# A recommendation tower (embedding gathers, pair products, three-layer MLP) on one core: GpSimd's gather loop unrolled, ids read in place, gathers released by pairs of feature groups

## What is computed

```python
e = jnp.stack([tbl_0[ids[:, 0]], tbl_1[ids[:, 1]], ..., tbl_25[ids[:, 25]]], axis=1)
combined = jnp.concatenate([dense[:, None, :], e], axis=1)         # (2048, 27, 128)
interactions = jnp.einsum('bfd,bgd->bfg', combined, combined)
iu, ju = jnp.triu_indices(27, k=1)
z = jnp.concatenate([dense, interactions[:, iu, ju]], axis=1)
h = jnp.concatenate([z, dense], axis=1)
h = jnp.maximum(h @ W_top1 + b_top1, 0.0)                          # 607 -> 512
h = jnp.maximum(h @ W_top2 + b_top2, 0.0)                          # 512 -> 256
y = h @ W_top3                                                     # 256 -> 1
```

## Time and profile before

| | |
|---|---|
| median of 3 runs | 739.69 us (738.09 to 743.75) |
| profiled execution, span | 741.8 us |
| TensorE matmuls busy | 462.5 us (62%), 3102 matmuls |
| VectorE, ScalarE busy | 240.0 us (32%), 271.2 us (37%) |
| GpSimd busy | 296.8 us (40%), 310 of its 317 instructions gathers |
| DMA | 34.56 MB, mean 47 GB/s |

### The profile page before, as it was taken

The page is one execution under the profiler, slowest core; times in us unless marked ns, Lnnn a source line. Parts: engine busy times, 40 slices in busy tenths (PEclk is TensorE's granted clock), DMA queues, the critical chain, the costliest instruction groups (busy, mean ns, idle before and its releaser), DMA issues.

```text
span 741.8 us, 9097 instructions
## 1 busy us (share of the span) xinstructions
PE 462.5 (62%) x3102; PEld 426.3 (57%) x3102; DVE 240.0 (32%) x697; ACT 271.2 (37%) x629; POOL 296.8 (40%) x317
## 2 busy tenths in 40 slices
PE   1327837482927649286683867658395592854987
PEld 1317727372927649175582857548294582842886
DVE  3216335240614215151331614315053340401441
ACT  2218322351605424062330714217051360614763
POOL 6760636345270543606245071622607147172000
PEclk9756958695967959578595886859677695875997
DMA  5564114211122111301012010230102212010000
GB/s 145 160 190 44 45 31 67 54 30 42 30 59 34 39 32 35 65 19 46 25 46 74 6 50 14 61 59 19 52 4 64 52 30 53 8 54 21 2 1 0
DMA packets 25437, 34.56 MB, mean 47 GB/s; under 512 B 9248, under 2 KB 18976, under 8 KB 25418
## 3 DMA queue, kind: packets, MB, share of 16 engines
q0 software_dynamic: 9920, 20.34, 10.3%
q1 hardware_dynamic: 15498, 13.97, 9.4%
HBM read 34.27 MB, written 0.01 MB: 46 GB/s over the span
## 4 chain that ended last, share of the span: by engine, by line
PE 52%; issue 26%; another core or an unknown queue 9%; ACT 7%; DMA 3%; DVE 2%; SPq 0%; ACTq 0%; DVEq 0%
PE gram_ps L428 17%; PE x_ps L411 15%; PE x_ps L388 4%; ACT x L608 4%; PE tail_ps L470 4%; PE tail_ps L472 3%; PE tail_ps L471 3%; DMA x<-in_tbl_dram 3%; PE tail_ps L501 2%; ACT gram L608 1%; PE tail_ps L464 1%; PE tail_ps L452 1%; DVE pairs L814 1%; ACT pairs L608 1%
## 5 line engine op out<-in xcount | busy, mean ns | idle before, releaser
L336 POOL DMA_INDIRECT rows<-in_tbl_dram,idx x266 | 252.4, 949 | 361.8 <-ACT idx L608 284.6
L428 PE MATMUL gram_ps<-x 128*128 128x108 f32 x1024 | 157.4, 299 | 83.4 <-issue 82.7
L428 PEld LDWEIGHTS gram_ps<-x 128*128 128x128 f32 x1024 | 146.2, 216 | 93.4 <-issue 93.2
L814 DVE COPY gram<-gram_ps 32x216 f32<-32x216 f32 x128 | 68.4, 534 | 346.3 <-remote 202.8
L411 PE MATMUL x_ps<-hot,table_hi 125*128 125x256 f32 x424 | 121.7, 334 | 89.4 <-issue 58.7
L608 ACT ACTIVATE gram<-gram_ps 32x216 f32<-32x216 f32 x128 | 68.8, 537 | 223.0 <-remote 162.5
L411 PEld LDWEIGHTS x_ps<-hot,table_hi 125*128 125x128 f32 x424 | 91.7, 227 | 99.8 <-issue 64.8
L838 DVE TENSOR_SCALAR hot<-ids_all,row_f 125x256 fp32r<-125x256 int32 x410 | 117.9, 356 | 36.4 <-remote 24.1
L411 PE MATMUL x_ps<-hot,table_lo 125*128 125x256 f32 x424 | 115.1, 318 | 17.3 <-issue 17.3
L411 PEld LDWEIGHTS x_ps<-hot,table_lo 125*128 125x128 f32 x424 | 91.1, 226 | 19.7 <-issue 19.5
L388 PE MATMUL x_ps<-ident,rows 128*128 128x128 f32 x320 | 60.9, 304 | 32.4 <-issue 18.6
(11 more groups left out here) (86 smaller groups left out, 435.0 us busy)
## 6 DMA issues: line engine op xcount, KB each, us to landing
ids_all<-in_selected_ids_dram SPq DMA_DIRECT2D x8, 640.0 KB
rows<-in_tbl_dram,idx POOLq DMA_INDIRECT x266
x<-in_tbl_dram SPq DMA_DIRECT2D x7, 500.0 KB
ids_all<-in_selected_ids_dram SPq DMA_DIRECT2D x8, 256.0 KB
rows<-in_r_dense_features_dram SPq DMA_DIRECT2D x16, 64.0 KB
w1p_raw<-in_W_top_dram SPq DMA_DIRECT2D x1, 702.0 KB
rows<-in_tbl_dram,ids_sb POOLq DMA_INDIRECT x38
gram<-in_W_top_dram SPq DMA_DIRECT2D x1, 512.0 KB
```

The lines of the kernel that those rows point to most:

```text
L336: pool.indirect_dma_start(out=dst, out_offset=None, in_=tables[table], in_offset=bass.IndirectOffsetOnAxis(ap=ids_t[:, table:table + 1], a ...
L428: last = pe.matmul(gram_ps[k % 2][:, i // PER_BANK, (i % PER_BANK) * SW:(i % PER_BANK + 1) * SW], x[t][:, a:a + PER, :], x[t][:, a:a + PER ...
L814: return dve.tensor_copy(dst, src)
```

## The change

`idx` and its copies on ScalarE go away, and with them `idx_ready` and `gathers_begun`: the gathers read `ids_sb` at the place of the tile. That needs a place known when the program is built, so GpSimd's loop is unrolled. Each pair of groups now has its own wait: groups 0 and 1 of macro tile m are gathered once TensorE has transposed group 1 of m - 1 in the same tile, groups 2 and 3 once it has transposed group 3, and the rest once it has transposed the last. SP's `load_dense` waits for group 0 instead of the last group. ScalarE's wait for the rest of the ids, ahead of its first join, goes too; GpSimd has it now.

```diff
-        idx = [sb(f"idx{t}", [P, NT], I32) for t in range(TILES)]
...
-                    sp.wait_ge(x_filled, x_before(m - 1, x_end(m - 1, t)))
+                    sp.wait_ge(x_filled, x_before(m - 1, x_use(m - 1, "rows", t, 0) + 1))
                     load_dense(m, t)
...
-            def gather(m, t):
-                if isinstance(m, int) and m == 0:
-                    pool.wait_ge(ids_loaded[0], 16)
-                    ids_t = ids_sb[:, t, :]
-                else:
-                    pool.wait_ge(idx_ready, (m - 1) * TILES + (t + 1))
-                    pool.sem_inc(gathers_begun, 1)
-                    ids_t = idx[t]
-                for g, features in enumerate(feature_groups[t]):
-                    for f in features:
-                        if f > 0:
-                            gather_table(rows[t][:, gathered_features.index(f), :], f - 1, ids_t, gathered[t][g])
+            def gather_group(m, t, g):
+                features = feature_groups[t][g]
+                if m < 2:
+                    pool.wait_ge(ids_loaded[min(m, 1)], 16)
+                if m > 0 and g % 2 == 0:
+
+                    later = min(g + 1, len(feature_groups[t]) - 1)
+                    pool.wait_ge(x_filled, x_before(m - 1, x_use(m - 1, "rows", t, later) + 1))
+                for f in features:
+                    if f > 0:
+                        gather_table(rows[t][:, gathered_features.index(f), :], f - 1, m * TILES + t, gathered[t][g])
...
-            for t in range(TILES):
-                gather(0, t)
-            with pool.Fori(1, NM - 1) as m:
+            for m in range(NM):
                 for t in range(TILES):
-                    gather(m, t)
-            gather(NM - 1, 0)
-
-            pool.wait_ge(joined[1], NM - 1)
-            pool.sem_inc(gathers_begun, 1)
-            gather_extra(0)
-            gather(NM - 1, 1)
-            gather_extra(1)
+                    for g in range(len(feature_groups[t])):
+                        gather_group(m, t, g)
+                    if m == NM - 1:
+                        if t == 0:
+
+                            pool.wait_ge(joined[1], NM - 1)
+                        gather_extra(t)
...
-                    if g == len(feature_groups[t]) - 1 and not is_last(m):
-                        index(m + 1, t)
-
-            def index(m, t):
-                copy(idx[t][:], ids_sb[:, m * TILES + t, :]).then_inc(idx_ready, 1)
...
-            act.wait_ge(ids_loaded[1], 16)
             join(0, 0)
```

More of the change, by code:

```diff
@@ L221, in dlrm_kernel @@
         w_lo_ready = sem("w_lo_ready")
-        idx_ready = sem("idx_ready")
         extra_gathered = [[sem(f"extra_gathered{t}_{g}") for g in range(len(extra_groups))] for t in range(TILES)]
-        gathers_begun = sem("gathers_begun")
         gathered = [[sem(f"gathered{t}_{g}") for g in range(len(feature_groups[t]))] for t in range(TILES)]
@@ L321, in _, with gather_table @@
         def _(pool):
-            def gather(m, t):
-                if isinstance(m, int) and m == 0:
-                    pool.wait_ge(ids_loaded[0], 16)
-                    ids_t = ids_sb[:, t, :]
-                else:
-                    pool.wait_ge(idx_ready, (m - 1) * TILES + (t + 1))
-                    pool.sem_inc(gathers_begun, 1)
-                    ids_t = idx[t]
-                for g, features in enumerate(feature_groups[t]):
-                    for f in features:
-                        if f > 0:
-                            gather_table(rows[t][:, gathered_features.index(f), :], f - 1, ids_t, gathered[t][g])
-            def gather_table(dst, table, ids_t, done):
+            def gather_group(m, t, g):
[8 more added lines that the diff above has]
+                        gather_table(rows[t][:, gathered_features.index(f), :], f - 1, m * TILES + t, gathered[t][g])
+            def gather_table(dst, table, tile, done):
                 pool.indirect_dma_start(
                     out=dst, out_offset=None, in_=tables[table],
-                    in_offset=bass.IndirectOffsetOnAxis(ap=ids_t[:, table:table + 1], axis=0)).then_inc(done, 16)
+                    in_offset=bass.IndirectOffsetOnAxis(ap=ids_sb[:, tile, table:table + 1], axis=0)).then_inc(done, 16)
             def gather_extra(t):
@@ L342, in gather_extra @@
                     for f in features:
-                        gather_table(extra_rows[t][:, extra_features.index(f), :], f - 1, idx[t], extra_gathered[t][g])
+                        gather_table(extra_rows[t][:, extra_features.index(f), :], f - 1, (NM - 1) * TILES + t,
+                                     extra_gathered[t][g])
             pool.iota(row_i[:], pattern=[[1, VC]], base=0, channel_multiplier=VC).then_inc(iota_ready, 1)
```

## The result

| | before | after |
|---|---|---|
| median | 741.72 us (738.09 to 744.59, 4 runs) | 656.0 us (650.97 to 660.74, 4 runs) |
| profiled span | 741.8 us | 648.2 us |
| ratio | | 0.883, 95% interval 0.8775 to 0.8884 |
| TensorE busy in the profiled span | 62% | 70% |

The forecast was 680 us, faster, by a shorter stall of TensorE beside the gathers. The profiled execution of the change is the quickest of its four (650.97 us), so the spans differ by 93.6 us, the medians by 85.7; what follows is worked out from the spans.

What follows compares the result with a forecast made beforehand. Bursts of gathers stalling TensorE were taken to bound the kernel. Savings of 45 (five loop periods), 6.5 (macro tile 0) and 9 (macro tile 6), 60.5 us, took 741.8 to 681.3, stated as 680; range 645 to 736.

Steps and rivals of the forecast that it cites:

- Undisturbed work is 55 us per macro tile: Loop period: 89.6 us less the two bursts' losses of 17 and 17.5 leaves 55 us of TensorE work.
- Copies, unrolling, dense loads, readers: 0.: Dropping idx copies (at most 2.9 us), unrolling GpSimd's loop, earlier dense loads and waits of gathered rows' readers: 0 each.
- Tile 0 in the loop: Its 19 gathers start at once as one burst, released at 27.0 us; TensorE loses 12.7, 4.3 less than before.
- an allowance of about 65, then a creep: Each gather burst: TensorE gets about 65 matmuls, then about 1 per us until 4.5 us after the last gather.
- Tile 1 in the loop: Gathers in pieces of 7, 8 and 4, the 7 and 8 joining: a loss of 12.3 us, period 80.0.
- a knife's edge: Tile 1: the allowance of 65 ends at 8 us, while group 3 is 64 matmuls on, deciding whether pieces join.
- Macro tile 0 and macro tile 6: Outside the five loop periods: macro tile 0 saves 6.5 us (28.5 lost to 22), macro tile 6 saves 9.
- The other signs: Wait of 3 to 5 us before the 4, release 4.5 us after last gathers, VectorE's "remote" waits down a fifth.
- Slow recovery: Between tile 1's pieces the allowance returns slowly: proportionally, 730 us (705 to 738: 0.15); not at all, 802 (slower: 0.08).
- Nearly free pieces: Creep starts near the seventh gather, so tile 1 loses 4 us, not 12.3: 647 us, chance 0.13 (640 to 660).
- No effect: TensorE's total stall goes with the number of gathers, 38 per macro tile, wherever they are: 740 us, chance 0.08.
- The rule that I quoted: A DMA never contends with a compute engine, so the gathers' place would be worth nothing: time near 740 us.

Runs made afterwards that it cites:

- e11_no_gathers_third: The changed kernel without gathers after macro tile 0 except the last macro tile's extra ones: 461.03 us beside 741.79 for the kernel before, ratio 0.6211.
- e12_even_pieces: The changed kernel with its six pieces of gathers per macro tile held apart by TensorE's steps: 611.23 us beside 740.83 for the kernel before, ratio 0.8268.
- e1_one_wait: The changed kernel with one wait per tile, on its last group's transposes: 454.62 us beside 453.46 for the kernel before, ratio 1.0044.
- e5_no_gathers: The changed kernel without gathers after macro tile 0 except six extra ones: 454.26 us beside 453.46 for the kernel before, ratio 1.0006.
- The second group: Four kernels run together on chip 4 (waits per group, pieces held back, plain DMAs from GpSimd or SP): 452.85 to 455.25 us beside 454.18 for the kernel before.
- the single one of 637.45 us: One of 19 executions of the unchanged kernel before in one group of runs: 637.45 us, where the other 18 took 449 to 462.
- e6_spread: The changed kernel with gather pieces held back until TensorE has done about 65 matmuls or more: 454.1 us beside 454.18 for the kernel before, ratio 1.0015.
- e7_pool_plain: The kernel before with each gather replaced by a plain DMA from GpSimd's queue: 452.85 us beside 454.18 for the kernel before, ratio 0.9952.

## Why the prediction was right, and where it was not

**What bounds the kernel.** Right for the executions it was made from. e11_no_gathers_third shows it directly: the stall goes when the gathers go, 741.79 to 461.03 us. What I could not see in one trace is that the stall is no part of the kernel: in other executions of the same program it is absent. "Undisturbed work is 55 us per macro tile" was too much; it is 50 (400 matmuls in 50 us). I had taken the parts beside the bursts as undisturbed, but some of them are spent catching up, at granted clocks of 0.81. The real loss was 89 - 50 = 39 us per period, not 34.5. This is the mis-sized term of the sum. The "about 10 and 9.4 us" for a burst's matmuls are the pace of the burst's own first 7.7 us and not that of the parts beside them, and those parts (116 matmuls in 16.4 us, 114 in 19.35) were taken as they stood. The loss before came out too small by 5 us, and so did the saving: with 49.6 us of undisturbed work and my own two losses of 12.7 and 12.3 the period is 74.6, and it measured 74.5.

**Copies, unrolling, dense loads, readers: 0.** Nothing in the rows contradicts this: GpSimd's pitch is still 1.25 us, and at the quick level the whole of the edit measures 1.0013.

**Tile 0 in the loop.** I forecast one burst of 19 without waits, from the second group's transposes on; the trace has it (207.81 to 232.35), and group 1 of tile 1 was done 34.3 us in, where I had 33.4. But the inside is not as described. I had the allowance last 12 us and then a creep, 80 to 85 matmuls by 27 us. In the trace TensorE stops dead 7 us in, after 41 matmuls, for 4.97 us, then runs on inside the same burst; it has made some 100 matmuls at 27 us and 110 at 236.8. I had named "more than 85" as a sign of being wrong, and here it is. So "an allowance of about 65, then a creep" is not a law of one burst, and "it is a number" fails: 41 after 7 us here, 67 after 11.3 us in the earlier trace rows. What stands out is that ScalarE and VectorE work beside TensorE here (19 and 21 instructions in the first 8.2 us, 5 and 4 in the burst of the earlier trace rows); that this is the cause is not shown. Nor does the release go with the length of the burst: 2.3 us after the last of these 19 gathers, 4.5 us after the 19 in the earlier trace rows.

**Tile 1 in the loop.** I had three cases at "a knife's edge": 9.1 for separate pieces, 12.3 for 15 + 4, and took 12.3, as the case nearest to the long burst of the trace. The trace shows separate pieces, 7, 8 and 4: the transposes of group 3 end at 249.20, in time for the 8 to follow, but GpSimd sees them only with the release. From the start of its first piece to the next period it takes 40.8 us (242.15 to 282.91), where I had 80.0 - 33.4 = 46.6: 5.8 less, all of the 5.5 us by which the mean period of 74.5 beats my 80.0. On my base of 55 us that reads as a loss of 6.5; but e11_no_gathers_third makes this part in 29.0 us and tile 0's in 20.6, so the change loses 11.8 us here and 34.3 - 20.6 = 13.7 in tile 0, catching up included. By that measure, the only one that rests on an undisturbed run, my 12.3 and 12.7 were near, and the 12.3 by luck, since it belongs to a case that did not come about.

**Macro tile 0 and macro tile 6.** 13.7 saved where I had 6.5: e11_no_gathers_third needs 39.9 us for macro tile 0, so the loss fell from 38.0 to 24.3, where I had 28.5 and 22, and again it is the loss before that was too small. Macro tile 6 saved 5.5 where I had 9; I did not take it apart. The start and the end gave 0.5 and 2.2, for which I had 0. By terms: 71.6 + 13.7 + 5.5 + 2.7 = 93.5, against 45 + 6.5 + 9 = 60.5. So the direction and the bounding stall were right, and a third of the saving was missing from the sum.

**The other signs.** The wait ahead of the 4 is 2.0 us, not 3 to 5; the release comes 2.3 to 2.9 us after the last gather, not 4.5; VectorE's "remote" waits fell by three quarters, not a fifth. The early burst of 19 and the separate pieces are there.

**The rivals.** Slow recovery: against it, the piece of 8 at 252.70 came 2.1 us behind the end of the piece of 7, and TensorE still made 55 matmuls from 250.00 to 258.90; e12_even_pieces, with pauses of 1.4 to 3.8 us between the pieces of a period, repeats it. Nearly free pieces (647) was the nearer case to the truth in size, and wrong in its reason: it let tile 1 lose 4 us, and tile 1 loses 6.5 on the same base, 11.8 against the undisturbed run. "No effect", with a stall that goes with the number of gathers, is refuted at the stalled level by the change and by e12_even_pieces, which have the same 310 gathers. The rule that I quoted (the Trainium skill, "SBUF — State Buffer", section "Who interferes with whom") needs two answers now. At the quick level the trace agrees with it: e1_one_wait and e5_no_gathers, with and without gathers, take the same time. At the stalled level the time that follows from the rule does not come out: 741.79 against 461.03. That is not to say that the engines and the DMAs meet in SBUF, for no run shows where the stall arises.

**What stays open: what the stall is.** The rows exclude the plainest causes. The gathers' data takes as long on both levels: on the queue of the gathers 10.3% of 741.8 us = 76 us in before, 16.7% of 453.8 us = 76 us in e1_one_wait:

```profile
q0 software_dynamic: 9920, 20.34, 10.3%
```

```profile
q0 software_dynamic: 9920, 20.34, 16.7%
```

A gather occupies GpSimd for 0.94 us in both, and a gram's copy takes VectorE 534 and 539 ns. What is held up is the start of instructions, also of matmuls that waited for nothing named, and the handing on from one engine to another, on all three compute engines at once. GpSimd's gathers keep their pitch, but its wait for transposes ends late too (252.70, above). Something counted over all of them would fit better than a number of matmuls. In the first full-pace stretch of a burst TensorE alone made 66 and 68 matmuls, 63 and 61 in the first two pieces of e12_even_pieces, but 41 in tile 0 of the change; matmuls, weight loads and the instructions of the other three together are 147 and 153, 137 and 148, and 129. That is closer, not equal; the piece of 8 from 245.18, with 73 matmuls before TensorE stands, fits neither count, and no run tests it. One place would give such a thing a mechanism: the Trainium skill, "NOTIFIC — the notification-queue block", section "Overflow: three behaviours, one of which stalls the engine", says that the block to which engines report events holds its producers back when its internal pipeline fills. No run here shows that this happens, and why it would come in some groups of runs only is just as open. The second group and e11_no_gathers_third ran on chip number 4 and met different levels, so even "a property of the chip" is not shown, only that the executions made together are on one level, the single one of 637.45 us excepted.

## What to carry to other kernels

Run the kernel before beside every variant, on more than one chip, ahead of explaining its trace: here the whole bottleneck, 39 of 89 us in each period, was absent in three of the five groups of runs. Where engines stall in step with bursts of indirect DMAs, and the gap is put down to "issue" and "remote", split the burst, and hold its pieces apart by steps of the engine that stalls. Here moving one burst and splitting the other gave 12%, and six pieces, those of 7 and 8 some 12 us ahead of the next, 17%, where the stall was there. Where it wasn't, the change cost nothing (1.0013), nor did the spacing of e6_spread (1.0015); e12_even_pieces was not run there. And take the undisturbed pace from a run without the disturbance, not from the stretches beside it: that was the error of this forecast.

## What the runs showed of the hardware that was not expected

- Two levels of one program, 741 and 454 us, with the same number of matmuls and gathers, the same time of the gathers' data, and the same durations of a gather and of a gram's copy. The lower level has TensorE busy 85% with gathers running without pause.
- At the upper level 266 gathers cost 281 us in long bursts (1.06 us each), though neither TensorE's undisturbed pace nor the time of the gathers' data differs. The engines are let go 2 to 3 us after the last gather of a piece of 7 or 8, 2.3 us after the 19 of the change, 4.5 us after the 19 in the earlier trace rows.
- The stop can end while the gathers go on (214.8 to 219.8 in the change).
- VectorE is busy a little longer where indirect gathers run without pause: 31.3 to 31.7 us per 50 us in e1_one_wait, 29.1 to 29.5 in e5_no_gathers on the same chip. With plain DMAs from GpSimd's queue in their place (e7_pool_plain) it is 29.1 to 29.5 too. It costs no time, as VectorE is far from full.
